# A new beginning, transition and order of tiles in a long-convolution and mixture-of-experts kernel

## What is computed

```python
kv = v[:, :, :, None, :] * x2[:, :, None, :, :]
y = irfft(rfft(kv, 2L) * rfft(k, 2L))[..., :L]
y = y + kv * skip
out = einsum('bhijl,bhil->bhjl', y, x1)          # x1 = x2 = ctx, v = layernorm(x)
x = x + out
```

```python
xf = layernorm(x)
scores = sigmoid(xf @ gate_w.T)                   # 8 experts, 2 taken per token
topk_w, topk_idx = top_k(scores, 2); topk_w = 2.5 * topk_w / sum(topk_w)
shared = (silu(xf @ swg.T) * (xf @ swu.T)) @ swd.T          # hidden width 704
h = silu(xf @ wg[e].T) * (xf @ wu[e].T); routed = h @ wd[e].T    # hidden width 352
x = x + shared + sum over the 2 of topk_w * routed
```

## Time and profile before

| | |
|---|---|
| median of 3 runs | 733.95 us (732.53 to 736.12) |
| the profiled execution | 733.79 us, of it a span of 732.0 us |
| mean granted clock of PE | 0.968 of full |
| busy: PE, DVE, ACT, POOL | 656.6 us (90%), 434.9 (59%), 294.7 (40%), 359.3 (49%) |
| DMA | 91.53 MB, mean 125 GB/s |
| PE's first matmul, and the start of its last | 14.34 us, 717.13 us |
| start of convolutions 1, 8, 13, 14 | 32.43, 95.06, 165.03, 177.69 us |
| PE passes its wait for the tile table | 481.74 us |

### The profile page before, as it was taken

How to read it: one execution, slowest core, us unless ns; L and a number is a source line. 1 busy time by engine, 2 the same in 40 slices (tenths; PEclk the granted TensorE clock), 3 DMA queues, 4 the chain that set the end, 5 groups by cost and what they waited for, 6 DMA issues and landing times.

```text
span 732.0 us, 11515 instructions
## 1 busy us (share of the span) xinstructions
PE 656.6 (90%) x3425; PEld 327.1 (45%) x3426; DVE 434.9 (59%) x714; ACT 294.7 (40%) x372; POOL 359.3 (49%) x296
## 2 busy tenths in 40 slices
PE   2889797969899999899999989986999999999991
PEld 1335242424344444344444443333555555555550
DVE  3799599685987695987886676773412112212210
ACT  4437558433223553233631367542523323323320
POOL 1799999764685355686564007400232232232222
PEclk9999899989999999999999998998999999999996
DMA  8933225203234710224214488698988888888843
GB/s 221 264 102 100 88 86 117 57 16 71 88 130 82 177 30 15 103 58 88 58 29 153 180 236 297 227 273 223 142 135 130 130 135 127 129 133 133 129 66 43
DMA packets 131668, 91.53 MB, mean 125 GB/s; under 512 B 98144, under 2 KB 111968, under 8 KB 131104
## 3 DMA queue, kind: packets, MB, share of 16 engines
q1 hardware_dynamic: 123312, 71.26, 39.5%
q0 software_dynamic: 8176, 18.75, 14.6%
q10 hardware_dynamic: 144, 1.05, 0.3%
HBM read 44.22 MB, written 25.65 MB: 95 GB/s over the span
## 4 chain that ended last, share of the span: by engine, by line
PE 49%; DVE 16%; POOL 12%; ACT 9%; DMA 5%; issue 5%; SPq 3%; POOLq 0%; DVEq 0%; ACTq 0%
PE banks L779 15%; PE banks L780 15%; PE banks L781 15%; POOL arena L640 7%; POOL arena L655 2%; DVE arena L1561 2%; DVE arena L1385 2%; DVE mixT L1392 2%; POOL arena L684 2%; DVE stats L1398 2%; DVE hm L1523 1%; ACT arena L1062 1%; ACT arena L1161 1%; DMA arena<-split_filters 1%; DMA out<-xf,ids 1%
## 5 line engine op out<-in xcount | busy, mean ns | idle before, releaser
L640 POOL TENSOR_TENSOR arena<-arena 128x512 f32<-128x512 f32 x124 | 141.7, 1174 | 64.4 <-ACT arena L1104 28.2
L742 POOL DMA_INDIRECT out<-xf,ids x39 | 61.1, 1567 | 194.6 <-DMA out<-xf,ids 139.6
L779 PE MATMUL banks<-arena 128*128 128x512 f16 x320 | 124.9, 390 | 19.4 <-DVE arena L1385 10.0
L780 PE MATMUL banks<-arena 128*128 128x512 f16 x320 | 124.6, 389 | 0.0
L781 PE MATMUL banks<-arena 128*128 128x512 f16 x320 | 124.4, 389 | 0.0
L779 PE MATMUL banks<-arena,normed 128*128 x312 | 98.5, 316 | 5.8 <-DVE hm L1711 5.8
L780 PE MATMUL banks<-arena,normed 128*128 x312 | 98.4, 315 | 0.0
L781 PE MATMUL banks<-arena,normed 128*128 x312 | 98.4, 315 | 0.0
L1385 DVE TENSOR_TENSOR arena<-banks,arena 128x512 f32<-128x512 f32 x128 | 81.3, 681 | 27.5 <-PE banks L781 27.1
L1709 DVE SCALAR_TENSOR_TENSOR hm<-banks,silu 128x256 f32<-128x256 f32 x39 | 16.5, 424 | 129.9 <-PE banks L781 129.9
L1062 ACT ACTIVATE arena<-arena 128x2048 f16<-128x2048 f32 x31 | 59.0, 1905 | 82.1 <-POOL arena L640 82.1
(11 more groups left out here) (186 smaller groups left out, 1053.2 us busy)
## 6 DMA issues: line engine op xcount, KB each, us to landing
arena<-split_filters SPq DMA_DIRECT2D x31, 256.0 KB, 3.3
arena<-in_expert_w SPq DMA_DIRECT2D x12, 544.0 KB, 7.9
stages<-in_expert_w SPq DMA_DIRECT2D x10, 544.0 KB, 4.7
arena<-in_ctx SPq DMA_DIRECT2D x8, 512.0 KB, 7.0
arena<-in_ctx_hidden SPq DMA_DIRECT2D x3, 1024.0 KB, 5.2
out<-x_tok SPq DMA_DIRECT2D x6, 512.0 KB, 6.2
x_tok<-in_expert_w SPq DMA_DIRECT2D x5, 544.0 KB, 6.1
mixT<-in_expert_w SPq DMA_DIRECT2D x5, 544.0 KB, 7.3
```

The lines of the kernel that those rows point to most:

```text
L640: nc.gpsimd.tensor_tensor(kv[s % 2][:, lb * COLS:(lb + 1) * COLS].rearrange("p (b j i) -> p b j i", i=NH, j=NH), v[:, a, None, :].to_broad ...
L742: nc.gpsimd.indirect_dma_start(out=out, out_offset=bass.IndirectOffsetOnAxis(ap=ids[slot][:, 0:1], axis=0), in_=yg[slot], in_offset=None, ...
L779: nc.tensor.matmul(dst, wh, xh, start=(k == 0), stop=False)
L780: nc.tensor.matmul(dst, wh, xl, start=False, stop=False)
```

## The change

It has five places. (1) **Beginning:** the loads of x go out first, half from SP's queue and half from ACT's; ctx_hidden goes from ACT's queue to SP's, behind them, and the small constants and the first filter from SP's to ACT's. Twenty matmuls on memset data stand at the head of PE's queue. -1/2 is memset, not loaded. DVE's `filter_low` and `first_filter_low` stand later, ACT's first copies and high parts alternate by tile, POOL's second product is made in eight half pieces that follow the four tiles (`second_outer`), and convolution 0 runs in two halves of 256 columns (`first_convolve`). (2) **Low parts:** `DVE_LOWS` has 6 and 8 in place of 7. (3) **Group 1** is reordered on DVE and PE. (4) **Transition:** gate/up 4 and 5 of group 2 stand around the four `mix_out` tiles, which now follow each other, `down` of group 2 has banks of its own and starts after the last product, gate/up 1 of the last group is split around `ranks`, the activation tables are loaded ahead, the order of experts is 0, 1, 2 with 2 as POOL's, `between` puts the pieces of experts 3 and 4 and half of 5 around the low parts, and `tile_table` stands behind the other half of expert 5. Loads of expert 5 and 6 stand in the loop over the pads and before the wait for the table; ids and expert 7 are loaded inside the first tiles, and ACT and DVE split expert 7 after tiles 3 and 4. (5) **Tiles:** the empty tiles come first, `tile_prev` and `tile_need` to match; gate and up alternate between banks 0, 1 and 2, 3, so `tile_gate_up(t)` waits for hm of tile t - 2, and the transposes of the last tiles go to bank 5.

```diff
-DVE_LOWS = (0, 1, 3, 5, 7, 9, 11) + tuple(range(2 * HG - 2, H, 2))
+DVE_LOWS = (0, 1, 3, 5, 6, 8, 9, 11) + tuple(range(2 * HG - 2, H, 2))
+WARM = 20
...
# SP
             for half in range(2):
-                for b2 in range(2):
-                    sp.dma_start(x_tok[0][b2 * RG:(b2 + 1) * RG, 2 * half:2 * half + 2, :],
...
-                if half == 0:
-                    sp.dma_start(con[:, 4 * P:CONST_W], consts[:, 4 * P:CONST_W]).then_inc(small_const_in, 16)
+                sp.dma_start(*first_rows(half, 0)).then_inc(first_x_in[half], 16)
             sp.dma_start(con[:, 0:P], consts[:, 0:P]).then_inc(const_in, 16)
-            sp.dma_start(filt_raw.bitcast(F32), first_filter).then_inc(first_filt_in, 16)
+            sp.dma_start(cT[0], ctx_hidden[0]).then_inc(cT_in[0], 16)
...
-            load_expert(5)
+                if e in (3, 5):
+                    load_expert(5, e - 3, e - 2)
+            load_expert(6)
...
             load_tile(1, 1)
-            load_expert(6)
...
-            for t in range(RING):
-                load_ids(t, t)
-            load_expert(E - 1)
...
# POOL
+            def second_outer(q):
+                pool.wait_ge(tokT_done, q + 1)
...
-            pool.wait_ge(tokT_done, Q)
-            outer(1)
+            for q in range(Q):
+                second_outer(q)
...
# PE
+            pe.wait_ge(warm_ready, 1)
+            for i in range(WARM):
+                nc.tensor.matmul(bank[0], hTl[:, 0, 0:P], hTl[:, 0, :], start=True, stop=True)
...
                 convolve(s0 + 4)
+                gate_up(g - 1, 2)
                 if g == 1:
                     skip_sum(1, 2)
                     skip_sum(1, 3)
-                gate_up(g - 1, 2)
-                if g < G - 1:
+                if 1 < g < G - 1:
                     prepare(g + 1, range(0, 2))
                 convolve(s0 + 5)
                 if g < G - 1:
+                    prepare(g + 1, range(2 if g > 1 else 0, Q if g > 1 else 2))
+                gate_up(g - 1, 3)
+                if g == 1:
                     prepare(g + 1, range(2, Q))
-                gate_up(g - 1, 3)
...
-            mix_out(G - 1, range(0, 2))
+            gate_up(G - 2, SM - 2)
+            mix_out(G - 1)
+            gate_up(G - 2, SM - 1)
+            pe.wait_ge(prod_done, LB * H)
             down(G - 2, 0)
-            mix_out(G - 1, range(2, Q))
...
-                if not isinstance(t, int) or t > 0:
-                    pe.wait_ge(r_hm, t)
+                if not isinstance(t, int) or t > 1:
+                    pe.wait_ge(r_hm, t - 1)
...
# DVE
+                link(nc.vector.scalar_tensor_tensor(out=t_no[:], in0=tile_no, scalar=float(-TILES),
+                                                    in1=n_end[:, E - 1:E].to_broadcast([1, SLOTS]), op0=ALU.add, op1=ALU.add))
...
-            filter_low()
             first_moments(0)
             first_moments(1)
             first_shift_by(0)
+            filter_low()
             first_shift_by(1)
-            first_filter_low()
             first_outer(0)
             first_outer(1)
+            first_filter_low()
...
+                    products(s0 + 3, 3, g, range(LB - 1, LB))
+                    total(s0 + 3, 3)
+                    skip_term(1, 0)
+                    skip_term(1, 1)
+                    gated(0, 1)
+                    skip_product(1, 2)
+                    skip_product(1, 3)
+                    pick(0)
+                    value_moments(2)
...
-                if m == SM - 1:
-                    tile_table()
...
+            expert(5, 2, 3)
+            tile_table()
...
-                if 2 <= t <= 3:
-                    expert(E - 1, *(first_half, second_half)[t - 2])
+                if t >= 3:
+                    expert(E - 1, *(first_half, second_half)[t - 3])
```

358 lines of the change are left out of this document (218 added, 140 removed).

## The result

The changed kernel took **740.08 us** (median of 6 runs, 739.02 to 741.8) against 734.28 for the kernel before, run on the same chip (732.53 to 736.12). The ratio is 1.0082, 95% interval 1.0061 to 1.0103. The profiled execution has a span of 738.1 us, and a mean granted clock of 0.958 where the old one had 0.968. The prediction was 718.7, range 706 to 727. It was wrong in sign.

The account below looks back on a forecast made before the run. PE, full from 207 us, was taken as the bound: its work, holes, half-clock time and two ends. Terms -7.8 - 4.4 + 3.5 - 1.6 - 4.8 = -15.1 took 733.8 to 718.7 us, range 706 to 727.

Parts of the forecast that it names:

- whatever the first 207 us lose or win goes through to the end: Whole kernel: since PE is full after 207 us, earlier gains or losses were said to reach the end.
- 1. The beginning: Start of the kernel: x loaded first and work reordered, so POOL's product for filter 1 ends earlier; -7.8 us.
- the bound of 11: Start: sign that the forecast is wrong, if ACT's first normalization comes later than 11 us.
- Everything in group 0 hangs on that: Group 0: ACT's high part, DVE's low part and convolution 1 all follow POOL's product for filter 1; 7.8 us earlier.
- Rival B: Start gives half, as x and ctx_hidden share DMA engines and the first product needs ctx_hidden; -4 there, 725.9 us; chance 0.17.
- 2. Low parts: Before convolution 8: POOL makes three low parts instead of four, DVE takes one more; -4.4 us, bounds -2.5 and -6.5.
- removed 5.1: Before convolution 8: POOL's mean time for one low part, 5.1 us, counted as saved when DVE takes it.
- 3. Group 1: Reordered group 1: 9 us of hole and slow clock go, new holes of 3, 3.4 and 4.5 come; about +3.5 us.
- Rival D: Group 1: POOL's late steps behind the inverse root all pass to PE, which loses 23 us; 735 to 738 us; chance 0.04.
- 4. Transition and entry: Group 2's end to tile 5: old waits go, new holes at table and tile 5; about -1.6 us, bounds -8 and +2.
- 5. The tail: End of the tile loop: empty tiles first, so the last scatter-add goes out at 719.1 instead of 723.9; -4.8 us.
- Wrong, if ... the clock is low for over 20 us after 100: After 100 us: sign that the forecast is wrong, if the clock is low for over 20 us.

Follow-up runs that it names:

- root late: Changed kernel with POOL's inverse root of group 1 moved behind product 15, instead of ahead of shared piece 8 and low part 13: 743.59 us, ratio 1.013.
- The first mend: Changed kernel with table ahead of expert 5's last pieces, expert 7's loads and splits as before, old low-part list and old group 1 order: 725.61 us, ratio 0.9869.
- the kernel with the later wait: Changed kernel with PE's wait for all 28 expert pieces at tile 9 instead of tile 5: 734.18 us, ratio 1.0004.

## Why the prediction was wrong, point by point

**What bounds the kernel.** The sentence that PE's holes and the slow clock are all there is was right, and its holes could all be found. What failed is the step from it: "whatever the first 207 us lose or win goes through to the end" was applied to gains that were no longer there at 207 (convolution 16: 207.2 before, 206.6 after). Of the 12.2 us that places 1 and 2 should have given at convolution 8 (near 83), 1.4 came (93.7), and the pieces of work moved at the entry opened holes that the sums had smaller or not at all.

**1. The beginning, -7.8 forecast, -4.9 at convolution 1, about -1.1 at the end.** The second statistics came at 8.56, at the late edge of the 7.5 to 8.5 forecast; ACT's normalization began at 10.43, within the bound of 11 that the prediction set:

```profile
8.56 1.28 DVE L1399 BATCH_NORM_STATS2 stats<-x_tok 128x6 f32<-128x512 f32 x2 [0.75 <-DMA x_tok<-in_x]
```

```profile
10.43 3.00 ACT L1134 ACTIVATE normed<-x_tok,shift,rstd 128x512 f32<-128x512 f32 x4 [4.35 <-DVE shift L1407]
```

POOL's eight half pieces ran as one chain of 6.27 us from 15.08 to 21.35, so they ended 2.6 us after the last copy (18.74), and 1.9 later than the 19.5 forecast:

```profile
15.08 6.27 POOL L663 TENSOR_TENSOR arena<-arena 128x256 f32<-128x256 f32 x8 [3.40 <-ACT arena L1118]
```

The failed step is the sentence "Everything in group 0 hangs on that", with 27.2 - 19.4 = 7.8 behind it: the lead of POOL's product was taken for the lead of PE, whose way to convolution 1 leads over convolution 0 and the skip sums (PE's rows above). With convolution 0 near 16, as forecast, and the 10.5 us that PE takes from there to convolution 1, this would have started near 26.5 even with POOL's product at 19.5, 5.9 earlier and not 7.8. After that POOL also hangs on DVE's var_eps and on whether DVE's low parts run beside its own, and 1.4 of the 4.9 us were left at convolution 8. Rival B was right in kind for the start (-4), from another cause than the one it named: DVE's first product in the changed kernel waits for PE's transposes (12.51), not for ctx_hidden. No gain was counted for the warm-up. The pairs show none that is clear: 727.36 without against 728.58 with, and 726.36 without against 724.42 with, one in each direction and both with intervals that overlap. PE takes 10.5 us from the start of convolution 0 to that of convolution 1 in all four.

**2. Low parts, -4.4 forecast, -0.7 measured.** The failed step is "removed 5.1". I followed the low part (6 and 8) taken off POOL, and not the one (7) put on it. It stands behind product 8, so PE waits 8.83 us before convolution 7. Where the 1.3 us of the sum come from, no row says. The price of a contended low part was right: number 7 took 6.58, where the prediction had 6.54.

**3. Group 1, +3.5 forecast, +2.9 and +2.5 measured.** Right (its own numbers, 177.4 - 177.7 + 3.6, give 3.3). The three holes are 2.81, 2.71 and 4.49, where the working had 3, 3.4 and 4.5; POOL's root came at 151.30 instead of 153.8, after 13.18 us of nothing:

```profile
151.30 1.01 POOL L682 TENSOR_TENSOR rstd<-var_eps,minus_half 128x4 f32<-128x4 f32 x1 [13.18 <-DVE var_eps L1476]
```

The chain over POOL to the second hole held too; what it lacked is the chain over DVE's shift and ACT's normalization, 1.26 us behind it (root late, above). Rival D, that these holes grow to 23 us, did not come.

**4. Transition and entry, -1.6 forecast, +12.9 in the profile (from convolution 28 to tile 6), about +8 by the runs (the sum below).** The hole of 2.90 went, but one of 2.73 came at 422.32, since PE's down product waits for gated 5, which DVE has behind an expert piece and the shift. The table's hole was 7.30 instead of 5.3: the pieces of expert 5 in front of it landed late (ACT waits for one until 474.28), so the table began at 478.18, not 474.7. ACT's row, then DVE's:

```profile
474.28 1.11 ACT L1213 ACTIVATE arena<-x_tok 128x1088 f16<-128x1088 f32 x1 [1.95 <-DMA x_tok<-in_expert_w]
```

```profile
478.18 0.15 DVE L1561 TENSOR_TENSOR n_f<-next_row,con 1x8 f32<-1x8 f32 x1
```

Tile 5's hole was 5.53 instead of 4.3. The waits for hidden rows were 3.00 and 1.97, where one of 1.8 was forecast. These four are some 9 us. The prediction had a transpose queue behind ids and a store, and not behind or beside expert 7's loads, which now go out at 511.23 and 517.02, among the tiles. A slip in the sum adds 3.0: from the first tile at 487.4 (+1.1) its own terms, -4.84, -0.9 and -2.3, then +4.3, +1.8 and +2.2, give +1.4 at tile 5, not -1.6. The clock was low as well, 0.83 over 71 us, which cost 5.4 us of PE's time more than in the kernel before, where the prediction had 2.2 for each of two holes. Expert 7's place had 4.3 + 1.8 + 2.2 = 8.3 in the sum, and undoing it gave back 10.6. What the rest of this place should have won came only in part (the sum, below).

**5. The tail, -4.8 forecast, -5.0 measured.** Right, in size and cause.

**The sum.** What was measured one at a time is -1.1 (beginning), -0.7 (low parts), +2.9 (group 1), -5.0 (tail), +10.6 (expert 7) and +0.6 (table): +7.3. The rest of place 4 (gate/up and mix tiles, order of the experts, two pairs of banks) was not measured alone. The first mend keeps it beside the beginning and the tail and took 9.4 us less than the kernel before, 3.3 more than these two alone. With these 3.3 the sum is +4.0. The whole measured +5.8. The parts were measured on different bases and each has an error of 1 to 3 us, so they need not add up closer than this. Between the forecast of -15.1 and the +5.8 lie 20.9 us. By these runs 9.5 of them are the transition and the entry (+7.9 instead of -1.6), 6.7 the beginning and 3.7 the low parts; group 1 takes back 0.6 and the tail 0.2. That is 19.1, and the missing 1.8 are the difference of the two sums.

**The chances.** 0.91 for faster rested on five terms that were read as if they were independent. Two of them shared POOL's queue, and the largest loss had no rival of its own: all rivals were about group 1 or the start. Rival D's 735 to 738 does not follow from its own terms: 15 us more than 718.7 is 733.7. And "Wrong, if ... the clock is low for over 20 us after 100" could tell nothing: after 100 us both kernels have a mean clock of 0.97, and a mean of 0.97 means 2 x 0.03 x 632 = 38 us at the low level in the kernel before too.

## What to carry to other kernels

Before an earlier engine is counted as a gain, ask what its consumer does until then: if the consumer is busy, the lead is not passed on. When a step moves into another stretch, date everything behind it in each in-order queue, its loads too, and not only the step's own use. The DMA engines' share times the length of a stretch gives a floor for that stretch and no more. And when a list decides which engine does which piece, look at what each engine was given as closely as at what it was relieved of.

## What the runs showed of the hardware

**POOL and DVE at once.** Of low part 7 on POOL the first of four subtractions took 3.24 us, while one of DVE's, 2.29 us, began at nearly the same time; the four alone take 4.50, 1.1 each. The rows:

```profile
81.73 3.24 POOL L677 TENSOR_TENSOR arena<-arena 128x512 f16<-128x512 f32 x1
```

```profile
81.67 2.29 DVE L1443 TENSOR_TENSOR arena<-arena 128x2048 f16<-128x2048 f32 x1 [2.38 <-ACT arena L1109]
```

3.24 - 1.1 is 2.1, nearly the whole of DVE's operation. DVE pays as well: its skip products took 1.39 and 1.55 us beside a POOL product and 0.75 alone (root late, above). By the Trainium skill, SBUF — State Buffer, Who interferes with whom, a DVE instruction with two SBUF inputs contends with a GpSimd one that reads SBUF; the traces agree. Products on POOL pay the same: 6.2 instead of 4.14 when they overlap (at 64.50 in the changed kernel, beside a DVE low part at 66.14).

**The clock after short holes.** In the changed kernel the matmul that follows the hole of 7.30 (at 483.37) is recorded with 0.61 us and the one after 3.00 (at 513.15) with 0.60, where the rows after 2.73 and 2.81 have 0.39 and 0.38. But the length of the hole does not settle it. After the 2.73 the eighth matmul has 0.63, and after a hole of only 1.97 (at 522.27) the fifth has 0.63; in the kernel with the later wait none of the nine after a hole of 3.61 (at 516.06) has more than 0.39. The entry's mean clock was 0.83 with 17.8 us of holes, and 0.94 or 0.91 with 12.0.

**Scatter-adds of one expert's tiles.** Issued 3.1 us apart, though one takes 5.1 us from issue to landing. The last four of the kernel before, each of which waited for the one ahead of it or for its rows, stood 5.3 to 5.9 apart.
